# Gated cross-attention block on one core: where the ffn result joins the residual, and when the next batch's first score tile is computed

## What is computed

```python
query = ctx @ Wq.T + bq ; key = ctx @ Wk.T + bk            # per batch, 512 x 128
attention = softmax(query @ key.T)                          # 512 x 512
x1 = x + tanh(g_xattn) * einsum("ln,mn->lm", layernorm(x), attention)
xn = (z - mean(z)) * rsqrt(var(z) + eps) * ln_weight + ln_bias      # z = layernorm(x1)
out = x1 + tanh(g_ffn) * ((xn @ sign(weight).T) * max|weight| * gamma + beta)
```

## Time and profile before

| | us |
|---|---|
| median of 3 runs | 123.74 |
| lowest, highest | 123.06, 123.81 |
| the profiled execution | 123.59 |
| its span in the trace | 121.8 |

### The profile page before, as it was taken

The page is one execution under the profiler, slowest core; times in us unless marked ns, Lnnn a source line. Parts: engine busy times, 40 slices in busy tenths (PEclk is TensorE's granted clock), DMA queues, the critical chain, the costliest instruction groups (busy, mean ns, idle before and its releaser), DMA issues.

```text
span 121.8 us, 1883 instructions
## 1 busy us (share of the span) xinstructions
PE 116.7 (96%) x565; PEld 94.7 (78%) x565; DVE 94.2 (77%) x186; ACT 86.5 (71%) x184; POOL 94.7 (78%) x108
## 2 busy tenths in 40 slices
PE   7799999999999999999999999999999999999980
PEld 6477887888887877878889888888888888888870
DVE  0159499999888996769966993799849948988991
ACT  3365999999997988476998795659987972245200
POOL 2046995869077998999995999994748999999970
PEclk9999999999999999999999999999999999999999
DMA  3999499833454400027871402457000012220045
GB/s 104 243 378 384 154 405 351 330 112 132 95 192 147 141 31 5 3 86 252 264 258 16 156 5 86 158 181 240 24 3 0 3 63 115 86 86 0 0 154 190
DMA packets 10394, 17.15 MB, mean 141 GB/s; under 512 B 1809, under 2 KB 2321, under 8 KB 10385
## 3 DMA queue, kind: packets, MB, share of 16 engines
q1 hardware_dynamic: 9808, 16.78, 39.9%
q10 hardware_dynamic: 576, 0.26, 0.8%
HBM read 12.59 MB, written 4.19 MB: 138 GB/s over the span
## 4 chain that ended last, share of the span: by engine, by line
PE 92%; DMA 4%; DVE 2%; issue 0%; SPq 0%
PE ps_y L420 37%; PE ps_ffn L433 23%; PE ps_score L355 7%; PE ps_turn L387 6%; DMA ctx_sb<-in_ctx_t_dram 4%; PE ps_score L387 3%; PE ps_y L387 3%; PE ps_ffn L325 2%; PE ps_turn L325 2%; PE ps_y L378 2%; PE ps_turn L355 1%; PE ps_score L364 1%; PE ps_ffn L334 1%; PE ps_y L497 1%; PE ps_ffn L449 1%; PE ps_y L343 1%
## 5 line engine op out<-in xcount | busy, mean ns | idle before, releaser
L915 POOL TENSOR_TENSOR xt_lo<-xt_raw,xt_hi 128x512 fp32r<-128x512 f32 x16 | 21.1, 1319 | 3.9 <-ACT xt_hi L561 2.9
L420 PE MATMUL ps_y<-pt_hi,xt_hi 128*128 128x512 f32 x64 | 18.1, 404 | 0.2 <-issue 0.2
L420 PE MATMUL ps_y<-pt_hi,xt_lo 128*128 128x512 f32 x64 | 17.5, 395 | 0.0
L420 PE MATMUL ps_y<-pt_lo,xt_hi 128*128 128x512 f32 x64 | 17.5, 395 | 0.0
L433 PE MATMUL ps_ffn<-w_sign,zt_hi 128*128 128x512 f32 x60 | 17.2, 408 | 0.0
L433 PE MATMUL ps_ffn<-w_sign,zt_lo 128*128 128x512 f32 x60 | 16.5, 396 | 0.0
L549 ACT ACTIVATE prob<-ps_score,neg_max 128x512 f32<-128x512 f32 x14 | 9.5, 681 | 9.7 <-DVE neg_max L698 9.6
L420 PEld LDWEIGHTS ps_y<-pt_hi,xt_lo 128*128 128x128 f32 x64 | 12.0, 188 | 2.9
L420 PEld LDWEIGHTS ps_y<-pt_lo,xt_hi 128*128 128x128 f32 x64 | 12.0, 188 | 2.9
L420 PEld LDWEIGHTS ps_y<-pt_hi,xt_hi 128*128 128x128 f32 x64 | 11.5, 188 | 2.6 <-issue 0.4
L433 PEld LDWEIGHTS ps_ffn<-w_sign,zt_lo 128*128 128x128 f32 x60 | 11.3, 188 | 2.8
(11 more groups left out here) (184 smaller groups left out, 270.2 us busy)
## 6 DMA issues: line engine op xcount, KB each, us to landing
xt_raw<-in_x_t_dram SPq DMA_DIRECT2D x16, 256.0 KB, 2.9
ctx_sb<-in_ctx_t_dram SPq DMA_DIRECT2D x8, 256.0 KB, 5.2
x_sb<-in_x_dram SPq DMA_DIRECT2D x8, 256.0 KB, 4.4
ctx_sb<-in_x_dram SPq DMA_DIRECT2D x8, 256.0 KB, 5.6
out_dram<-x SPq DMA_DIRECT2D x8, 256.0 KB, 2.0
out_dram<-ctx_sb SPq DMA_DIRECT2D x7, 256.0 KB, 2.1
w_raw<-in_weight_t_dram SPq DMA_DIRECT2D x4, 256.0 KB, 7.0
ln_w<-in_ln_weight_dram SPq DMA_DIRECT2D x1, 256.0 KB, 6.3
```

The costliest lines, as they stand in the source:

```text
L420: mm = pe.matmul(ps_y[t % 2][:, :], lhs[:, t, k, :], rhs[:, k, :], start=(k == 0 and i == 0), stop=(k == KN - 1 and i == 2))
L915: nc.gpsimd.tensor_tensor(xt_lo[:, t, :, :], xt_raw[:, t, :, :], xt_hi[:, t, :, :].bitcast(f32), ALU.subtract).then_inc(xt_lo_done, 1)
```

## The change

For batches 0 to 2, `scale_ffn` writes its product back into its PSUM bank and counts a new semaphore `ffn_scaled`; VectorE waits for that semaphore and for `x1b_done`, and then adds the bank to x1 itself. `ffn_evac`, which releases the bank to TensorE, is now counted by this addition. GpSimd's four `add_ffn` a batch leave `back`, the stores wait for `ffn_evac` in their place, and VectorE's wait for `out_done` is gone. Batch 3 is done as before. On TensorE the three products of `scores(b+2, 0)` are issued behind `turn_ffn(b,3)` and ahead of `attend(b+1, 0)`, with waits for tile 0 of `pt_hi` and `pt_lo` (they are read from the bank which the scores overwrite); they no longer begin `back(b+1)`. Only `back(0)` keeps its `scores(1,0)` at the start, and `back(2)` has none.

```diff
@@ store, SyncE
-                sp.wait_ge(out_done, T * b + t + 1)
+                if b == B - 1:
+                    sp.wait_ge(out_done, 1)
+                else:
+                    sp.wait_ge(ffn_evac, 1 + T * b + t + 1)
@@ back, TensorE
-                scores(b + 1, 0)
+                if is_first(b):
+                    scores(b + 1, 0)
                 attend(b, 1)
...
                 turn_ffn(b, 3)
+                if b + 2 < B:
+                    pe.wait_ge(pt_hi_done, T * (b + 1) + 1)
+                    pe.wait_ge(pt_lo_done, T * (b + 1) + 1)
+                    scores(b + 2, 0)
                 attend(b + 1, 0)
                 feed(b, 3)
@@ scale_ffn, VectorE
-                if b > 0:
-                    dve.wait_ge(out_done, T * (b - 1) + t + 1)
-                nc.vector.scalar_tensor_tensor(out=ffn[:, t, :], in0=ps_ffn[(t + 1) % 2][:, :],
-                                               scalar=rstd2[:, t:t + 1], in1=gain[:, :],
-                                               op0=ALU.mult, op1=ALU.mult).then_inc(ffn_evac, 1)
+                bank = ps_ffn[(t + 1) % 2]
+                if b == B - 1:
+                    nc.vector.scalar_tensor_tensor(out=ffn[:, t, :], in0=bank[:, :],
+                                                   scalar=rstd2[:, t:t + 1], in1=gain[:, :],
+                                                   op0=ALU.mult, op1=ALU.mult).then_inc(ffn_evac, 1)
+                else:
+                    nc.vector.scalar_tensor_tensor(out=bank[:, :], in0=bank[:, :],
+                                                   scalar=rstd2[:, t:t + 1], in1=gain[:, :],
+                                                   op0=ALU.mult, op1=ALU.mult).then_inc(ffn_scaled, 1)
+                    dve.wait_ge(ffn_scaled, T * b + t + 1)
+                    dve.wait_ge(x1b_done, T * b + t + 1)
+                    nc.vector.tensor_tensor(x1_buf[b % 2][:, t, :], x1_buf[b % 2][:, t, :], bank[:, :], ALU.add)\
+                             .then_inc(ffn_evac, 1)
@@ back, GpSimd
-                add_ffn(b, 0)
                 add_shift(b, 3)
-                add_ffn(b, 1)
                 split_xt(b + 1, 2)
-                add_ffn(b, 2)
                 split_xt(b + 1, 3)
-                add_ffn(b, 3)
```

More of the change, by code:

```diff
@@ L191, in flamingo_block_kernel @@
         last_scaled = sem("last_scaled")
+        ffn_scaled = sem("ffn_scaled")
         last_out_done = sem("last_out_done")
@@ L296, in _ @@
             sp.dma_start(out[B - 1, P:2 * P, :], x1_buf[(B - 1) % 2][:, 1, :]).then_inc(out_stored[(B - 1) % 2][1], 16)
-            sp.wait_ge(out_done, T * (B - 1) + 2)
+            sp.wait_ge(out_done, 2)
             sp.dma_start(out[B - 1, 2 * P:3 * P, :], x1_buf[(B - 1) % 2][:, 2, :])\
```

## The result

| | us |
|---|---|
| changed kernel, median of 4 runs | 125.11 (124.85 to 125.32) |
| before, beside it, median of 4 | 123.72 (123.06 to 123.81) |
| ratio, 95% interval | 1.0128 (1.0096 to 1.0161) |
| profiled execution, its span | 124.92, 123.1 |

The kernel is 1.3% slower: 1.39 us between the medians, where 1.60 was forecast; the time named was 125.2, the time measured is 125.11.

The account below looks back on a forecast made before the run. TensorE was taken to bound the kernel. Stage terms 0.02 + (0.16 + 0.11 + 0.15) + 1.16 = 1.60 us, added to the profiled 123.59, gave 125.2; the range was 123.4 to 126.0.

Parts of the forecast that it names:

- TensorE's stream sets the end, and only its gaps count: TensorE, busy 116.7 of 121.8 us: only its idle time can be saved, and any new wait lengthens the time one for one.
- The gap of 0.42: TensorE's wait ahead of the attention at 45.89, end of stage 0: covered by moved scores, then taken back, leaving +0.02 us.
- rival 1: Ends of the stages: `centre` is not held by GpSimd's `add_shift`; shift +0.27 us, time 123.9; chance 0.20.
- The pair costs 0.73: VectorE's scale plus addition: 1.38 us in place of 0.65 per tile, 12 tiles; bank released at 1.46 instead of 0.74.
- The wait ahead of feed (b,2): TensorE waiting for the later bank release: 0.16 to 0.18 us in stages 1 and 2, under 0.2 and swallowed in stage 0.
- The wait of 0.11 ahead of turn (1,3): End of stage 1: the turn waits for `centre`, starting at 70.78, and TensorE's shift grows from 0.18 to 0.29 us.
- the price of 0.10: Time from VectorE's end to TensorE's start, read at the attention at 45.89 and used six times: 0.10 us.
- `centre` of (b,3) is held by `add_shift`: VectorE, ends of stages 1 and 2: `centre` ends 0.55 us behind GpSimd's `add_shift`, taking 1.55 instead of 0.74.
- Stage 2 has no scores to cover the wait: Attention of batch 3 starts at 97.40 against 95.80; TensorE's shift grows from 0.44 to 1.60 us, a term of 1.16.
- rival 2: Whole kernel: not slower, the gain of 0.42 us stays and nothing added comes to light; 123.2; chance 0.12.
- Rival 3: VectorE's addition is held by GpSimd as `centre` is, up to 0.3 us more for each of three pairs; 126.0; chance 0.10.
- What costs nothing: Removing 12 additions of 1.3 us from GpSimd, earlier stores, and `row_max` left in place: no effect on TensorE's waits.

Follow-up runs that it names:

- experiment 2: The kernel before with only the first scores moved on TensorE, nothing else changed: 123.44 us, 0.9996 of the kernel before.
- experiment 7: The kernel before with the scores moved and GpSimd's `split_xt` (b+1,2) put ahead of its addition of tile (b,1): 123.45 us, 0.9983 of the kernel before.
- experiment 3: The changed kernel with GpSimd's `add_shift` of tile (b,2) moved behind `power2` (b,1), in stages 0 to 2: 124.16 us, 1.0050 of the kernel before.
- experiment 8: The changed kernel, but tile 0 of each batch scaled into SBUF and added by GpSimd at stage end: 123.64 us, 1.0009 of the kernel before.
- Experiment 1: The changed kernel with the first scores back at the start of TensorE's stage, additions still on VectorE: 126.08 us, 1.0203 of the kernel before.
- experiment 6: The changed kernel with VectorE adding in batch 2 only, GpSimd in batches 0 and 1, scores still moved: 124.70 us, 1.0093 of the kernel before.
- experiment 4: The changed kernel with the scale written to SBUF, releasing the bank at once, and VectorE adding from SBUF: 126.75 us, 1.0262 of the kernel before.
- experiment 5: The changed kernel with VectorE adding in batches 0 and 1 only, GpSimd in batch 2, scores still moved: 124.01 us, 1.0037 of the kernel before.

## Why the prediction was right, and where its steps were off

*TensorE's stream sets the end, and only its gaps count.* Right: in every run the shift at attention (3,0) is that of the last product within 0.02, and GpSimd's 18 us bought nothing by themselves.

*The gap of 0.42 is covered, and taken back by `centre` of (1,0).* Right in what is left of it, to 0.01 (+0.03 for +0.02): GpSimd's two splits from 51.32 are back to back, and `centre` took 1.24. The gain itself was shown by experiments 2 and 7, with -0.42 at that point. One step on the way was wrong. The wait for the bank ahead of feed (0,2), 0.24, was to be swallowed by the end of the stage, and it wasn't: with the scores in between, the attention waits for nothing that could hide it. So at attention (1,1) TensorE had gained 0.23 and not 0.42 (the prediction's rival 1 does subtract this wait). It didn't reach the sum only because turn (1,0) hangs on `centre`: TensorE waited 0.25 there instead of 0.44.

*The pair costs 0.73 and releases the bank 0.72 later.* Right: 67.66 is 0.79 after 66.87, the next instruction 0.60 later, so 1.39 for the pair; the bank is free 1.48 after the scale's start. The wait ahead of feed (b,2) was mis-sized: 0.16 to 0.18 in the prediction. The addition of tile (1,0) ended at 68.35 and the feed began at 68.49, so 0.14 and not 0.10 from end to start. From feed (1,1) to feed (1,2) are 2.54 (65.95 to 68.49) where before 2.32 (66.21 to 68.53), and from feed (2,1) to (2,2) 2.56 (91.33 to 93.89) where before 2.32 (91.18 to 93.50): 0.22 and 0.24.

*The sum.* Measured in the same steps it reads 0.03 + (0.07 + 0.22 - 0.01 + 0.20) + 1.14 = 1.65, where 0.02 + (0.16 + 0.11 + 0.15) + 1.16 was worked out. The 0.07 had no term: nearly all of it is one step, as the products behind turn (1,0), which had waited, began 0.42 after it instead of 0.36. It is also the whole error of 0.07 at attention (2,0). That attention starts 0.10 behind the end of `pt_lo` at 71.59, and `pt_lo` stands behind `centre` and `add_shift`; `add_shift` began 34.41 after feed (0,0), 0.07 later than the 34.34 worked out (68.84 - 34.50). The larger wait for the bank isn't in it. The wait of 0.11 ahead of turn (1,3) didn't come: the turn is 0.94 behind the rows ahead of it (69.50 to 70.44), as before (69.55 to 70.49). TensorE was later there than worked out, and a turn begins 0.05 behind the end of `centre` (54.44 to 54.49), not 0.10. So the price of 0.10, read at one place and used for all, was right for the attention, too high for the turn and too low for the feed (0.14).

*`centre` of (b,3) is held by `add_shift`, 1.55 instead of 0.74.* Right: 1.53, twice. That this, and not the pair's length alone, makes the greater part was shown by experiment 3: with VectorE's order untouched and `centre` at 0.74, 1.10 of 1.65 goes. The rest, 0.55, is left with the pair, and that trace shows where: 0.21 and 0.24 are waits for the bank ahead of feeds (1,2) and (2,2), 0.10 is the wait for `pt_lo` ahead of attention (3,0), which starts 0.46 after its turn. The pair is also what made `centre` late enough to be second, and experiment 8 shows both at once: without it in that one place nothing is left of the loss. The two parts can't be added as if they were apart; each alone is partly covered by TensorE's slack.

*Stage 2 has no scores to cover the wait.* Right: 1.14 of the 1.65 come there, 1.24 us from turn to attention instead of 0.36. Experiment 1 turned stage 1 into a second stage 2, experiment 6 had the loss in stage 2 alone.

*Rivals.* Rival 1 (`centre` isn't held) and rival 2 (all is hidden) fell with the rows of 1.53. Rival 3 (the addition is held) fell with 686 to 689 ns; experiment 4 shows what it would have been with a second SBUF input. The rule of the Trainium skill (SBUF — State Buffer, "Who interferes with whom"), that one SBUF input isn't touched and two are, agrees with the traces on both sides: 0.69 beside GpSimd with one, 0.78 to 1.67 with two.

*Under "What costs nothing" the prediction has the removal of GpSimd's additions.* That was too simple, and its own stages 0 and 1 don't treat it so. The relief sets who is first: once GpSimd isn't held itself, it comes to `add_shift` before VectorE comes to `centre`. And without the relief the moved scores would have met a late `xt_lo` (experiment 2).

*The time.* 123.59 + 1.60 = 125.2 came nearer to 125.11 than its working deserves. The shift in the trace was 1.66, 0.06 more than the sum; the medians differ by 1.39, and by 1.52 against the 22 executions of the kernel before that ran beside experiments 1 to 4. Executions reach feed (0,0) up to 0.9 us apart (below), and four runs a side may not average that out; this is likely, not shown.

## What to carry to other kernels

Where one engine's stream fills the span, first write down its few gaps, then each wait it will meet and by how much; an addition to another engine costs the time nothing until it stands ahead of one of those waits, and one place in a stage can carry the whole loss. Ask for each wait what follows it: a later one may hide it, and here one that was thought hidden wasn't. Relieving an engine also changes who is first at what two engines share: ask for each instruction with two SBUF inputs which GpSimd operation will now have begun before it. Move independent work of the full engine to the place ahead of its tightest wait, and look at what then becomes the next late thing.

## What the runs showed that I had not expected

- The second operand's place decides: an addition of two SBUF tensors took 0.78 to 1.67 us where it began beside a 128x512 operation of GpSimd (eight of twelve), the same with one operand in PSUM 0.686 to 0.689, beside it or not. The detour of scaling in the bank is what keeps the addition out of the contention, and moving it out cost 1.6 us.
- An instruction that comes second doesn't pay the other's full length plus its own: each of the five `centre` that were held in the changed kernel ended 0.54 to 0.55 behind GpSimd's end (53.89 to 54.44, 69.84 to 70.39), not 0.74.
- Who is held is not quite who starts second in the record. In the kernel before, `centre` started at 101.59 and GpSimd's next operation, back to back with the one ahead of it, at 101.65; `centre` was held until that one's end, 102.94, and 0.55 more. So it was with starts 0.02 to 0.04 apart in experiments 2, 5 and 7. In experiment 4, 0.07 ahead (71.20 and 71.27), `centre` took 0.74 and `add_shift` 1.83. The 0.31 of the changed kernel (68.55 and 68.86) are well beyond this.
- Executions of nearly the same code reach feed (0,0) at 34.13 to 35.00 us. In the kernel before, TensorE stood 0.66 us waiting for the context's load near the start; that isn't all of it, as the execution with 35.00 has no such wait. A difference of 0.4 us between two single profiles can be this alone; counted from feed (0,0), the traces mostly compare within some 0.1 (experiment 5 stood 0.2 off on VectorE and GpSimd).
